# Causal attention: the mask as a minimum on VectorE's exponentials instead of triangle products on TensorE

## The reference, cut to what matters

```
q, k, v = (heads(Wq, bq), heads(Wk, bk), heads(Wv, bv))
q = _apply_rope(q, cos, sin)
k = _apply_rope(k, cos, sin)
att = jnp.einsum('bhqd,bhkd->bhqk', q, k) * (1.0 / np.sqrt(D))
causal = jnp.tril(jnp.ones((T, T), bool))
att = jnp.where(causal[None, None], att, NEG_BIG)
att = jax.nn.softmax(att, axis=-1)
y = jnp.einsum('bhqk,bhkd->bhqd', att, v)
```

## Time and profile before

| what | value |
|---|---|
| median of 3 runs | 2900.57 us (2889.88 to 2901.99) |
| the profiled execution: own time, span of its trace | 2906.91 us, 2905.1 us |
| mean granted TensorE clock | 0.868 of full |
| busy: PE, PEld | 2219.8 us (76%), 1129.1 us (39%) |
| busy: DVE, ACT, POOL | 1964.1 us (68%), 1538.1 us (53%), 1212.0 us (42%) |
| line 479, maxima on DVE, all three calls | 806.0 us busy |
| line 892, exponentials on ACT, all three calls | 744.9 us busy |

### The profile page before, as it was taken

How to read it: one execution, slowest core, us unless ns; L and a number is a source line. 1 busy time by engine, 2 the same in 40 slices (tenths; PEclk the granted TensorE clock), 3 DMA queues, 4 the chain that set the end, 5 groups by cost and what they waited for, 6 DMA issues and landing times. The chain is left out here.

```text
span 2905.1 us, 48985 instructions
## 1 busy us (share of the span) xinstructions
PE 2219.8 (76%) x17390; PEld 1129.1 (39%) x17406; DVE 1964.1 (68%) x3710; ACT 1538.1 (53%) x3073; POOL 1212.0 (42%) x1268
## 2 busy tenths in 40 slices
PE   6999988886898995664827778777523877888886
PEld 2333334453444443554702333333223872323232
DVE  7888857675566653653258888888762227888884
ACT  4788862122566662331446766666321224767775
POOL 5423204343443401332446776676573434532310
PEclk9999987787999996776968898999856997999998
DMA  3111210000212112003830000000014971223110
GB/s 118 29 41 31 49 55 1 1 1 3 47 31 50 33 26 63 22 23 129 280 92 0 0 0 1 1 1 1 0 41 150 297 237 34 37 43 56 37 31 16
DMA packets 127627, 152.81 MB, mean 53 GB/s; under 512 B 19993, under 2 KB 108761, under 8 KB 126777
## 3 DMA queue, kind: packets, MB, share of 16 engines
q1 hardware_dynamic: 120792, 136.12, 17.4%
q0 software_dynamic: 6592, 13.56, 1.3%
HBM read 96.15 MB, written 25.59 MB: 42 GB/s over the span
## 5 line engine op out<-in xcount | busy, mean ns | idle before, releaser
L479 DVE TENSOR_REDUCE a_mx<-banks 128x2 f32<-128x1024 f32 (+3 forms) x768 | 806.0, 1087 | 235.6 <-PE banks L1051 131.5
L892 ACT ACTIVATE a_prob<-banks 128x512 f32<-128x512 f32 (+3 forms) x1536 | 744.9, 541 | 268.1 <-PE banks L1089 144.8
L1116 PE MATMUL banks<-a_prob,a_vaug 128*32 128x256 f32 (+2 forms) x5632 | 433.7, 389 | 0.2
L2225 POOL TENSOR_TENSOR m_hc<-m_h,m_cs 128x512 f32<-128x512 f32 x256 | 332.5, 1321 | 131.6 <-DVE m_h L2090 131.0
L1089 PE MATMUL banks<-a_Qs,a_Ks 64*128 64x512 bf16 (+3 forms) x1536 | 325.8, 365 | 47.9 <-DMA a_Qs<-a_negm 25.6
L2090 DVE TENSOR_TENSOR_SCAN m_h<-banks,m_u 128x512 f32<-128x512 f32 x256 | 301.0, 1209 | 21.1 <-issue 21.1
L1042 PE MATMUL banks<-a_Ks,a_Qs 63*128 63x512 bf16 (+3 forms) x1536 | 286.0, 369 | 35.5 <-DVE a_mx L479 28.6
L2373 PE MATMUL banks<-m_hc,kc 128*128 128x512 f32 x512 | 290.8, 652 | 9.6 <-DVE m_yf L2207 8.5
L2281 ACT ACTIVATE banks<-m_dt,acoef 128x512 f32<-128x512 f32 x256 | 174.9, 689 | 137.3 <-DVE m_h L2090 136.4
L1042 PEld LDWEIGHTS banks<-a_Ks,a_Qs 63*128 63x128 bf16 x1536 | 74.3, 93 | 330.0 <-issue 164.6
L1116 PEld LDWEIGHTS banks<-a_prob,a_vaug 128*32 128x32 f32 x5632 | 119.0, 109 | 156.1 <-issue 115.1
(11 more groups left out here) (434 smaller groups left out, 4181.5 us busy)
## 6 DMA issues: line engine op xcount, KB each, us to landing
c_wbuf<-in_w2e SPq DMA_DIRECT2D x71, 512.0 KB
b_wbuf<-in_w1e SPq DMA_DIRECT2D x39, 578.0 KB
a_Ks<-a_parts SPq DMA_DIRECT2D x252, 64.0 KB
a_Qs<-a_parts SPq DMA_DIRECT2D x252, 64.0 KB
rows_in<-in_unused SPq DMA_DIRECT2D x1, 4579.5 KB, 18.5
c_yb<-rows_in SPq DMA_DIRECT2D x71, 64.5 KB
a_mixed_in<-rows_back SPq DMA_DIRECT2D x16, 256.0 KB, 4.4
a_Qs<-a_negm SPq DMA_DIRECT2D x192, 2.0 KB
```

The costliest lines, as they stand in the source:

```text
L479: dve.tensor_reduce(both[:, :, c], m_bank(u)[:, :, 0:keys[c % NT]], AX.X, ALU.max).then_inc(S("m_read"), 1)
L892: act.activation(prob[:, n % DEEP, first_query[kt]:T], s_bank(u)[:, first_query[kt]:T], ACT.Exp, scale=scale).then_inc(S("s_read"), 1)
L1116: i = pe.matmul(V[32 * hl:32 * hl + 32, q0:q1], vaug[:, b % 3, kt, g % NG * GH + hl, :], prob[:, (4 * a + hl) % DEEP, q0:q1], start=kt == ...
L2225: gp.tensor_tensor(hc[:, n % 6, :], h[:, n % 4, :], cs[:, k % 4, :], ALU.mult).then_inc(S("weighed"), 1)
```

## The change

Only the causal call changes. The four triangle products of each pair of scores go (the tables with them). A new program on VectorE, `vector_mask`, takes the minimum of the diagonal 128 x 128 blocks of four heads' exponentials, in place, with a table `keep1` that holds 0 where the key is later than the query and 3e38 elsewhere; its due time is 4a + 5.2 for the four slots from 4a on, and it waits for the exponential of slot 4a + 3. The values wait for it and stand at 4a + 9.6 and 11.6 instead of 6.5 and 8.5; `prob` has 16 buffers; the copy of line 922, `oturn`, `oback`, `out` and the store move by 3 slots. The maxima keep their triangles.

```
--- before.py
+++ after.py
 PACK_B = [("wq", 128), ("wk", 128), ("wv", 128), ("wo", 128), ("cols", 2), ("bv", 128), ("bo", 128),
           ("g1", 128), ("be1", 128), ("wg", 8), ("ids", 32)]
...
-           ("maxL0", 128), ("maxL1", 128), ("scoreL0", 128), ("scoreL1", 128),
-           ("cornQ", 512), ("cornK", 512), ("maxR0", 64), ("maxR1", 64), ("scoreR0", 64), ("scoreR1", 64),
+           ("maxL0", 128), ("maxL1", 128), ("cornQ", 512), ("cornK", 512), ("maxR0", 64), ("maxR1", 64),
            ("cornL", 128)]
...
+            deep = DEEP + 4 if causal else DEEP
...
-                vaug, prob = room("vaug", [P, 3, NT, H, 32]), room("prob", [P, DEEP, T])
+                vaug, prob = room("vaug", [P, 3, NT, H, 32]), room("prob", [P, deep, T])
...
-                select = prob[:, DEEP // 2:, :].rearrange("p a t -> p (a t)").bitcast(BF16).rearrange(
+                select = prob[:, deep - 6:, :].rearrange("p a t -> p (a t)").bitcast(BF16).rearrange(
                     "p (n i h m) -> p n i h m", n=2, i=3, h=H // 2)
...
+                behind = 3.0 if causal else 0.0
                 m_at = {("max", g, c): max_at(g, c) for g in range(NGB) for c in range(8)}
-                m_at.update({("oturn", g): 32 * g + 38.2 for g in range(NGB // 2)})
+                m_at.update({("oturn", g): 32 * g + 38.2 + behind for g in range(NGB // 2)})
                 m_at.update({("v", b): begin(b) + 24.2 for b in range(B)})
-                m_at.update({("out", b): 64 * b + 78.2 for b in range(B)})
+                m_at.update({("out", b): 64 * b + 78.2 + behind for b in range(B)})
...
-                s_at.update({("oback", b): 64 * b + 74.7 for b in range(B)})
+                s_at.update({("oback", b): 64 * b + 74.7 + behind for b in range(B)})
...
+
+                def vector_mask(dve):
+                    for a in range(16 * B):
+                        q0 = first_query[a % NT]
+                        yield 4 * a + 5.2
+                        s_done(dve, ("score", 4 * a + 3))
+                        own = prob[:, 4 * a % deep:4 * a % deep + 4, q0:q0 + P]
+                        dve.tensor_tensor(own, own, keep.unsqueeze(1).broadcast_to([P, 4, P]),
+                                         ALU.min).then_inc(S("p_masked"), 1)
...
-                        if n >= DEEP and n % 4 == 0:
-                            act.wait_ge(S("av_done"), (n - DEEP) // 4 + 1)
+                        if n >= deep and n % 4 == 0:
+                            act.wait_ge(S("av_done"), (n - deep) // 4 + 1)
                         s_wait(act, u)
-                        act.activation(prob[:, n % DEEP, first_query[kt]:T], s_bank(u)[:, first_query[kt]:T],
+                        act.activation(prob[:, n % deep, first_query[kt]:T], s_bank(u)[:, first_query[kt]:T],
                                        ACT.Exp, scale=scale).then_inc(S("s_read"), 1)
...
-                        yield 32 * g + 36.0
+                        yield 32 * g + 36.0 + behind
...
                     if store is not None:
-                        yield 64 * b + 82.0
...
                             s_free(pe, u)
-                            i = pe.matmul(s_bank(u)[:, q0:T], Ks[lo:lo + HALF, b % 4, pair, kt * P:(kt + 1) * P],
-                                          Qs[lo:lo + HALF, b % 4, pair, q0:T], start=True, stop=not causal)
-                            if not causal:
-                                i.then_inc(S("s_written"), 1)
-                        if causal:
-                            for par in range(2):
-                                pe.matmul(s_bank(("score", n + par))[:, q0:q0 + HALF], tri_table("scoreL0", HALF * par),
-                                          tri_table("scoreR0", HALF * par), start=False, stop=False)
-                            for par in range(2):
-                                pe.matmul(s_bank(("score", n + par))[:, q0 + HALF:q0 + P], tri_table("scoreL1", HALF * par),
-                                          tri_table("scoreR1", HALF * par), start=False, stop=True).then_inc(S("s_written"), 1)
+                            pe.matmul(s_bank(u)[:, q0:T], Ks[lo:lo + HALF, b % 4, pair, kt * P:(kt + 1) * P],
+                                      Qs[lo:lo + HALF, b % 4, pair, q0:T], start=True, stop=True).then_inc(S("s_written"), 1)
 
                 def tensor_values(pe):
                     for a in range(16 * B):
...
                         for half, (q0, q1) in enumerate(spans):
-                            yield 4 * a + 6.5 + half * (0.05 if kt == NT - 1 else 2.0)
+                            yield 4 * a + (9.6 if causal else 6.5) + half * (0.05 if kt == NT - 1 else 2.0)
                             if half == 0:
-                                s_done(pe, ("score", 4 * a + 3))
+                                if causal:
+                                    pe.wait_ge(S("p_masked"), a + 1)
+                                else:
+                                    s_done(pe, ("score", 4 * a + 3))
                                 if kt == 0:
                                     if g % NG == 0:
                                         m_done(pe, ("v", b))
...
-                                              prob[:, (4 * a + hl) % DEEP, q0:q1], start=kt == 0 and half == 0 and g % 2 == 0,
+                                              prob[:, (4 * a + hl) % deep, q0:q1], start=kt == 0 and half == 0 and g % 2 == 0,
                                               stop=kt == NT - 1 and g % 2 == 1,
...
+                    lanes["vector"].append(vector_mask)
 
                 if mixed:
...
 
             attention_all("a1_", xres, (wa("wq1"), wa("wk1"), wa("wv1"), wa("wp1"), c1[:, 0:1], c1[:, 1:2], wa("bv1")),
-                          scale, causal=True,
+                          scale, causal=True, keep=wa("keep1"),
...
-    left = {name: np.zeros((n, P)) for name in ("maxL0", "maxL1", "scoreL0", "scoreL1")}
+    left = {name: np.zeros((n, P)) for name in ("maxL0", "maxL1")}
-    right = {"maxR0": later.copy(), "maxR1": later.copy(), "scoreR0": later.T.copy(), "scoreR1": later.T.copy()}
+    right = {"maxR0": later.copy(), "maxR1": later.copy()}
-    left["scoreL0"][r[1:], r[1:]] = 1
-    left["scoreL0"][0, n:] = 1
-    right["scoreR0"][0] = NEG
-    left["scoreL1"][r, n + r] = 1
+        "keep1": np.where(np.arange(P)[:, None] > np.arange(P)[None, :], 0.0, 3e38).astype(np.float32),
```

More of the change, by code:

```diff
@@ L345, in rep, with attention_all @@
             return piece.unsqueeze(1).broadcast_to([P, NT, C])
-        def attention_all(tag, xres, w, scale, causal=False, corners=False, swapped=None, double=None, bo=None,
+        def attention_all(tag, xres, w, scale, causal=False, keep=None, corners=False, swapped=None, double=None, bo=None,
                           load=None, store=None, mixed=None, gated=None):
+            deep = DEEP + 4 if causal else DEEP
             wq, wk, wv, wo, bq, bk, bv = w
@@ L1007, in sync_batch @@
                     if store is not None:
-                        yield 64 * b + 82.0
+                        yield 64 * b + 82.0 + behind
                         m_done(sp, ("out", b))
```

## The result

| what | before | after |
|---|---|---|
| median | 2896.91 us (9 runs) | 2912.38 us (9 runs) |
| ratio | | 1.0058, 95% interval 1.0044 to 1.0071 |
| span of the profiled execution | 2905.1 us | 2911.4 us |
| mean granted TensorE clock | 0.868 | 0.871 |
| PE, DVE, POOL busy | 2219.8, 1964.1, 1212.0 us | 2191.7, 2063.6, 1227.7 us |

The change costs 0.58%, some 16 us. The same stretch of the causal call as in the earlier trace rows, with its header; behind it the five whole periods from GpSimd's second start to its seventh, first of the kernel before, then of the one after. (PEclk is the mean granted clock of TensorE. The trace has only two levels, full, 2.4 GHz, and half of it, so a value between 0.50 and 1.00 is a mix of both.)

A forecast was written before the change was run, and what follows sets the result against it. Bound: each batch's chain of GpSimd and transfers, 34.1 us. Six batches at 4.9 us delay less 1.0 gain, less 0.3 for the ends, give +23 us: 2,924 us against the 2,900.6 median, range 2,889 to 2,944.

The forecast's parts named there:

- The bound: In each causal batch, 34.1 us of GpSimd and transfers set the length; TensorE waits for the third group's maxima row.
- The cost of a minimum: On VectorE: lowest 0.63 us, highest 3.06 beside a GpSimd operation, since each waits until the other is done.
- The walk: One batch followed through GpSimd's run: VectorE's maximum for the second group's row 6.6 us late, SyncE's row 5.4 late.
- Winning back on SyncE: Between the second and third groups' rows, 0.5 us of the delay is recovered, leaving the third group 4.9 us late.
- The gain between the third group's score and the last projection: On TensorE, six pairs lose triangles (0.4 us) and half of the values moves out (0.57): 1.0 us gained a batch.
- TensorE's wait of 3.48: TensorE's wait for the third group's maxima row, 3.48 us in one batch, stays about as it is.
- The period: Starts of GpSimd's line 848, one a batch, come 52 us apart instead of 48.4.
- the ends: Outside the six delayed batches: last 96 slots -1 us, last minimum in the tail +0.7, together -0.3.
- covered minimum: Rival: minima find gaps beside GpSimd, or SyncE recovers the late row; -6 us, 2,895 us; chance 0.22.
- TensorE pays out: Rival: the row wait is slack of SyncE's order, so TensorE's 17 us come off; 2,884 us; chance 0.13.
- Later still: Rival: nothing is won back and GpSimd's longer run meets a sixth minimum before the row; +37 us, 2,938; chance 0.07.

The follow-up runs named there:

- the move and the clock: The kernel before with values and what follows three slots later, sixteen buffers, and eight matmuls ahead of the third group's wait, no minimum: ratio 0.9958.
- the mirror: The kernel before with values moved and minima only in the stretch where GpSimd works (36 of 128), triangles elsewhere: ratio 1.0084.
- the kernel with neither mask: The kernel before with values moved and the scores' triangles left out, no minimum, so causal exponentials are unmasked: ratio 0.9994.
- the one-input kernel: The changed kernel with each minimum replaced by a VectorE reduction of the same exponentials to a spare tile, one SBUF input: ratio 0.9952.
- the hybrid: The kernel before with values moved and minima only outside GpSimd's stretch, triangles inside it: ratio 0.9981.
- the move alone: The kernel before with only values and what follows three slots later and sixteen buffers; triangles kept, no minimum: ratio 0.9983.

## Why the prediction was right, and where it was off

**The bound** was read rightly: a chain of GpSimd and transfers sets the batch. The triangles' 17 us on TensorE bought nothing (the kernel without them: 0.9994), and what did shorten the time lies elsewhere: the move and the clock (0.9958), neither of which takes a product away.

**The cost of a minimum** was the right step: 0.68 by itself and up to 2.54 beside GpSimd (forecast 0.69 and near 3), GpSimd's operations up to 2.81 (forecast 2.8 to 3.1). One detail was the other way round: the first minimum doesn't come before GpSimd's first operation but waits 1.9 us for it. The mean of all minima is 0.94, below the forecast 1.1 to 1.4, since only 32 of the 128 are held for long and none of those outside GpSimd's run is.

**The walk** gave the decisive maximum 6.6 us late; it is 5.2 late in the batch traced, and the row 4.0 late in the mean instead of 5.4. The waits that it added up were 5.6; measured are 1.86 + 0.70 + 1.58 + 0.58 + 0.47 = 5.2 over six minima. The idle time of VectorE that was used up was taken as 2.5; it is 3.2 (five waits for maxima, 2.5, and one of 0.7 for the values) of which none is left after. These two are 1.1 of the 1.4 us. That the negated maximum no longer waits behind ScalarE's copy, 1.2 us, was forecast rightly.

**Winning back on SyncE** was taken as 0.5. From one row to the next it is 34.2 - 19.4 = 14.8 us after and 30.0 - 15.4 = 14.6 before in the mean, so nothing is won back; the 15.9 of the batch that I read was the longest of the six. Delay 4.2 instead of 4.9.

**The gain between the third group's score and the last projection** was the term most mis-sized: 1.0 forecast, 2.0 measured. At full clock the stretch takes 13.1 us with nothing changed in it, 12.4 with the move and 12.2 with the change. The half of the values is thus worth 0.7 (forecast 0.57) and the triangles 0.2 (forecast 0.4). The rest is the clock, which the prediction had not counted: late minima shorten TensorE's wait, and the granted clock behind it was 0.87 or 1.00 instead of 0.77 to 0.87. By difference, an estimate, it was worth about 2.0 - 0.9 = 1.1 us a batch in the mean. For the same reason TensorE's wait of 3.48 did not stay about as it is, as forecast: all such waits together went from 22.6 us in 8 to 12.6 in 6.

**The period** is 50.0 us instead of the 52 forecast. With 4.2 and 2.0 in place of 4.9 and 1.0 the sum is 11.1 + 4.1 + 0.7 - 0.5 = +15.4 against +23. The forecast also gave the last batch the gain, which it does not have, and took the ends as -0.3, where the first period brought 0.5 and the tail cost 0.7. In the median, 2,924 against 2,912.4, another 3.7 us come from the median of before: 2,900.6 of three executions, 2,896.9 of nine. So the mechanism and the way were right and the size was one and a half times too large, by a delay and a gain that were both off in the same direction.

The rival "covered minimum" is excluded by the profile after and by the mirror, "TensorE pays out" by the kernel with neither mask. "Later still" had one thing right, that nothing is won back on SyncE, but its later row and its longer run of waits did not come.

The Trainium skill's rule of "SBUF — State Buffer", section "Who interferes with whom", held here in both directions: a minimum waits for the end of the GpSimd operation under way, and line 859 takes 0.45 us more behind one. The same page says that a VectorE instruction with at most one SBUF input, outside its two-port modes, does not contend with GpSimd; the one-input kernel shows that with 128 operations, none above 0.69 us.

## What to carry to other kernels

Before work moves to an engine with idle time, look at what runs beside it and how many inputs the new instruction reads from SBUF: 61% busy said that VectorE had room, and 36 of 128 instructions in the wrong place cost more than all gained. Work taken off an engine that is waiting for a chain only lengthens its wait, and on TensorE it can cost a slower clock behind it; then a few matmuls inside the wait are worth more than a thousand removed. Ask for each stretch which transfer ends the wait, and place what two engines share outside of its chain.

## What the runs showed of the hardware that I had not expected

The size of the clock's effect after short idle times. The same instructions take 13.1 us at a granted clock of 1.00 and 15.1 at 0.77. With neither mask the clock of the next 15 us was 0.71 after waits of 3.4 to 3.8 us, in five batches of five. In the one-input kernel it was 1.00 after waits of 1.15 and 1.65, 0.76 after 1.70 and 1.98 and 0.88 after 2.91. The length of the wait alone does not decide it, though: the hybrid had 0.70 after 1.51, the move alone 1.00 after 2.06, and the kernel before 0.87 after 3.48. What else decides it these runs don't show; eight matmuls ahead of the wait gave 1.00 in all five batches. And VectorE's minimum that has to wait shows the wait as its own length: in the profile it looks like a slow instruction, not like idle time, so the busy share of 89% contains it.
